# Issuing the loads of the keys ahead of the reciprocals' store and load in step 4 of the first layer

## The chip, the cores and the metric

The program runs on one core of one Trainium2 chip. The metric is the device time of one execution in microseconds; the median of a few executions is given. The core has five instruction queues that run side by side: TensorE (PE), VectorE (DVE), ScalarE (ACT), GpSimd (POOL) and SyncE (SP). SP here only issues DMA transfers and waits on semaphores. Each queue runs its own instructions strictly in order.

## The reference

Two transformer layers run one after the other on x of shape (8, 512, 128), each with a modulation from a small vector c. The first layer, in which the change lies, is an attention with 16 heads of 8 elements, followed by a routed feed-forward block:

```python
mod = (_silu(L0_c) @ L0_wmod).reshape(8, 6, 1, -1)      # sa, ca, ga, sb, cb, gb
h = _layernorm(x) * (1 + ca) + sa
latent = h @ Wc_down
q = (latent @ Wq_up).reshape(B, T, 16, 8)
k, v = split(latent @ Wkv_up)                           # one key/value head of 8, shared by all 16
att = softmax(causal(einsum('bthd,bsd->bhts', q, k) / sqrt(8)))
y = einsum('bhts,bsd->bthd', att, v).reshape(B, T, 128)
x = x + ga * (y @ Wc_proj)
h = _layernorm(x) * (1 + cb) + sb
x = x + gb * experts(h)          # 8 experts, each takes its 1024 best tokens
```

The second layer is a windowed attention (64 tokens) and a gated token-mixing block. All inputs and outputs are float32.

## The kernel before

The attention of the first layer is a software pipeline over the 8 batch rows. Every engine runs the same double loop, `for n in range(-2, 9)` and, inside, `for s in range(10)`; n is a pass, s a step. In pass n, row n has its scores, exponentials and products with the values computed, one 128x128 block of (queries, keys) in each of the ten steps. At the same time row n+1 has its maxima finished, row n+2 is projected to queries and keys, and row n-1 has its outputs normalised, projected and added to X.

[...]

- **Queries and keys of row n+2.** PE projects the queries in step 1 and the keys in step 2 (`q`, `k` in `misc`, L485 and L488). Each is cut into three bf16 parts by ACT, DVE and POOL (tiles `qs` and `ks`). In step 3 SP stores both to DRAM (`d_q<-qs` L1102, three transfers; `d_k<-ks` L1106, four). In step 4 ACT issues the three loads of the queries (`Q<-d_q`, L666, 384 KB each) and SP the three loads of the keys (`K<-d_k`, L1143, 24 KB each). The two sets count on one semaphore, `q_in`. PE waits for it before the first product of the maxima of that row (L462), which stands at the start of step 8 of the same pass.
- **Maxima of row n+1.** PE multiplies Q and K (L462, with the mask L469), DVE reduces (L798). In step 6 PE transposes the result (L496), DVE cuts it into parts `ms` (L763 to L767), SP stores it (`d_m<-ms` L1163), waits until the store has landed, and loads it as three rows of Q (`Q<-d_m` L1167). PE waits for these rows (`m_in`) before the first scores of the next pass (L423).
- **Sums of row n-1.** SP loads the sums of the exponentials (`lc<-d_y` L1121) and the outputs (`yt<-d_y` L1123) in step 0. DVE takes reciprocals in step 3 (`rc`, L905). In step 4 SP stores them (`d_r<-rc` L1130), waits until the store has landed (L1131), and loads them spread over the partitions (`rl<-d_r` L1132). POOL multiplies in step 6 (`yn`, L1053), PE projects near the end of step 8 (`pj`, L501), DVE adds to X (L770) and, in passes up to 4, takes the statistics of row n+3 (L739). From these POOL makes the normalised row (L1014, L983), which PE transposes in step 0 of the next pass (L480).
- **Outputs of row n.** ACT copies them out of PSUM (L637) after steps 0, 2, 5 and 9; SP stores each copy in the step after (`y_store`, L1088). In steps 1, 3 and 6, and in step 0 of the next pass, there is such a store; in step 4 there is none.

The order on SP is the order in which its loop is written. In step 4 of passes 1 to 5 it is: the reciprocals' store, the wait, the reciprocals' load, then a wait for the keys' stores (`k_st`) and the three loads of the keys. Passes -2 to 0 have keys to load but no reciprocals; passes 6 and 7 have reciprocals but no keys. In step 5 SP loads `cb` (L1154), in step 6 it does an outputs' store and the transfers of the maxima.

Of the kernel before, what the change touches and what calls it, by code (L numbers as in the profile page):

```python
# [27 lines left out]
NB, T, D = 8, 512, 128  # L28
NT = T // P
NTILE = NB * NT  # L30
NH, DH = 16, 8
# [8 lines left out]
PARTS = 3  # L40
# [4 lines left out]
QB = 3  # L45
# [136 lines left out]
def program(nc, ctx, ins, out):  # L182
# [3 lines left out]
    def sem(name):  # L186
        return ctx.enter_context(nc.semaphore(name))
# [7 lines left out]
    def sb0(name, shape, dt=F32):  # L195
        return a0.enter_context(nc.sbuf_tensor(name, shape, dt))

    def dram(name, shape, dt):
        return nc.dram_tensor(name, shape, dt, kind="Internal").ap()
# [3 lines left out]
    d_k = [dram(f"d_k{i}", [PARTS, DH, T], BF16) for i in range(2)]  # L203
# [58 lines left out]
    K = [sb0(f"K{i}", [P, T], BF16) for i in range(QB)]  # L262
# [57 lines left out]
    DS = {n: sem("a0_" + n) for n in dnames}  # L320
# [42 lines left out]
    def bc(ap, shape):  # L363
        return ap.to_broadcast(shape)
# [704 lines left out]
    def sync_part(sp):  # L1069
# [11 lines left out]
        def y_store(Y):  # L1081
            b, g = divmod(Y, NT)
            sp.wait_ge(S["y_ev"], Y + 1)
            if g == 0 and b >= 2:
                sp.wait_ge(DS["yt_in"], 16 * (b - 1))
                sp.wait_ge(DS["lc_in"], 16 * (b - 1))
            for j in range(4):
                sp.dma_start(d_y[b % 2][4 * j:4 * j + 4, :, P * g:P * g + P].rearrange("h d q -> d h q"),  # L1088
                             ysb[Y % 2][32 * j:32 * j + DH + 1, :].rearrange("p (h q) -> p h q", q=P)
                             ).then_inc(DS[f"y_st{Y % 2}"], 16)  # L1090

        for n in range(-LEAD, NB + TAIL):
            for s in range(NSTEP):
                t = NSTEP * n + s
                b = n + 2
                if 0 <= b < NB and s == 3:
                    par = b % 2
                    sp.wait_ge(S["q3_rdy"], b + 1)
                    if b >= 2:
                        sp.wait_ge(DS[f"q_in{par}"], QIN * (b // 2))  # L1100
                    for a in range(PARTS):
                        sp.dma_start(bass.AP(d_q[par].tensor, a * D * T, [[T, NH], [NH * T, DH], [1, T]]),  # L1102
                                     qs[:, a, :]).then_inc(DS[f"q_st{par}"], 16)
                    sp.wait_ge(S["k3_rdy"], b + 1)
                    for i in range(NT):
                        sp.dma_start(bass.AP(d_k[par].tensor, P * i, [[T, DH], [DH * T, PARTS], [1, P]]),  # L1106
                                     ks[32 * i:32 * i + DH, :, :]).then_inc(DS[f"k_st{par}"], 16)
                if 0 <= t - 1 < NSTEP * NB:
                    b, ps = divmod(t - 1, NSTEP)
                    g, i = STEPS[ps]  # L1110
                    if g == i and b < LB:
                        y_store(NT * b + g)
                b = n - 1
                if 0 <= b < LB and s == 0:
                    for par in range(2):
                        sp.wait_ge(DS[f"y_st{par}"], 64 * 2 * (b + 1))
                    if b >= 1:
                        sp.wait_ge(S["rc_rdy"], b)
                        sp.wait_ge(S["yn_rdy"], b)
                    y = d_y[b % 2]  # L1120
                    sp.dma_start(lc[:, :], bass.AP(y.tensor, DH * T, [[(DH + 1) * T, NH], [64, T // 64], [1, 64]])  # L1121
                                 ).then_inc(DS["lc_in"], 16)
                    sp.dma_start(yt[:, :], bass.AP(y.tensor, 0, [[(DH + 1) * T, NH], [T, DH], [1, T]])  # L1123
                                 ).then_inc(DS["yt_in"], 16)
                if 0 <= b < LB and s == 4:
                    sp.wait_ge(S["rc_rdy"], b + 1)
                    if b >= 2:
                        sp.wait_ge(DS["rl_in"], 16 * (b - 1))
                    r = d_r[b % 2]
                    sp.dma_start(r.rearrange("h (a q) -> (h a) q", q=64), rc[:, :]).then_inc(DS["r_st"], 16)  # L1130
                    sp.wait_ge(DS["r_st"], 16 * (b + 1))  # L1131
                    sp.dma_start(rl[:, :], bass.AP(r.tensor, 0, [[T, NH], [0, DH], [1, T]])).then_inc(DS["rl_in"], 16)  # L1132
                if (n, s) in LIMIT_ROWS:
                    i = LIMIT_ROWS.index((n, s))
                    sp.wait_ge(s_eye, 1)
                    sp.dma_start(K[i][NPR:P, :], KC[:, :]).then_inc(s_kc[i], 16)
                    sp.dma_start(Q[i][P - QW:P, :, :], bc(QC[:, :].unsqueeze(1), [QW, NH, T])).then_inc(s_kc[i], 16)
                b = n + 2
                if 0 <= b < NB and s == 4:
                    par = b % 2  # L1140
                    sp.wait_ge(DS[f"k_st{par}"], 64 * (b // 2 + 1))
                    for c in range(PARTS):
                        sp.dma_start(K[b % QB][24 * c:24 * c + 24, :],  # L1143
                                     bass.AP(d_k[par].tensor, c * DH * T, [[0, PARTS], [T, DH], [1, T]])
                                     ).then_inc(DS[f"q_in{par}"], 16)
                if n == -1 and s == 3:
                    sp.wait_ge(s_modR, 2)
                    sp.dma_start(d_cb, modR[:, 0, 2 * D:5 * D]).then_inc(DS["cb_st"], 16)
                if 0 <= n < NB and s == 5:
                    if n == 0:  # L1150
                        sp.wait_ge(DS["cb_st"], 16)
                    if n >= 2:
                        sp.wait_ge(S["h2_rdy"], n - 1)
                    sp.dma_start(cb[n % 2][:, :, :].rearrange("p a d -> p (a d)"),  # L1154
                                 bass.AP(d_cb.tensor, 3 * D * n, [[0, P], [1, 3 * D]])).then_inc(DS[f"cb_in{n % 2}"], 16)
                b = n + 1
                if 0 <= b < NB and s == 6:
                    par = b % 2
                    sp.wait_ge(S["m_rdy"], b + 1)
                    if b >= 2:  # L1160
                        sp.wait_ge(DS[f"m_in{par}"], 48 * (b // 2))
                    for a in range(PARTS):
                        sp.dma_start(bass.AP(d_m[par].tensor, a * NH * T, [[QW, NQB], [4 * T, NHG], [T, 4], [1, QW]]),  # L1163
                                     ms[:, a, :]).then_inc(DS["m_st"], 16)
                    sp.wait_ge(DS["m_st"], 16 * PARTS * (b + 1))
                    for a in range(PARTS):
                        sp.dma_start(Q[b % QB][NPR + a:NPR + a + 1, :, :], d_m[par][a:a + 1, :, :]  # L1167
                                     ).then_inc(DS[f"m_in{par}"], 16)
                if (s == 7 and 0 <= n - 2 < LB - 2) or (n, s) in ((LB, 4), (NB, 0)):
                    b = n - 2  # L1170
                    sp.wait_ge(S["misc_free"], M0.full(("h2", b)))
                    sp.dma_start(d_hT[:, T * b:T * b + T], h2T[:, :]).then_inc(DS["h_st"], 16)
                if 0 <= n < NB and s == 9:
                    for dst, src in late_weights[n::NB]:
                        sp.dma_start(dst, src, allow_slow_non_contiguous=True).then_inc(s_lw, 16)
                    if n == 0:
                        sp.dma_start(d_acc.rearrange("(i p) d -> p i d", p=P),
                                     bc(zrow[:, :].unsqueeze(1), [P, NTILE, D])).then_inc(s_lw, 16)
                b = n - 2
                if 0 <= b < LB and s == 9:  # L1180
                    sp.wait_ge(S["tab_rdy"], b + 1)
                    sp.dma_start(d_tab[T * b:T * b + T, :].rearrange("(i p) f -> p i f", p=P),
                                 tab[:, :, :]).then_inc(DS["tab_st"], 16)
# [38 lines left out]
    g.zrow, g.biti, g.bitf = zrow, biti, bitf  # L1222
    g.WT, g.GG, g.WPG, g.WVG, g.BPG, g.m1, g.gmean = WT, GG, WPG, WVG, BPG, m1, gmean
    stages = [(tensor_part, scalar_part, vector_part, gpsimd_part, sync_part), moe(nc, ctx, g)]
    mid.close()
    stages.append(block1(nc, ctx, g, out))
# [1260 lines left out]
```

## Time and profile before

| | us |
|---|---|
| median of 3 runs | 889.79 |
| lowest and highest | 885.54 and 890.29 |
| the profiled execution | 883.99 |
| its span, first to last instruction | 882.2 |

| engine | busy us | share |
|---|---|---|
| PE | 730.6 | 83% |
| DVE | 561.2 | 64% |
| ACT | 450.2 | 51% |
| POOL | 400.6 | 45% |

The attention of the first layer fills the span up to about 380 us; the experts follow up to about 640 us, then the second layer. A wait is listed by the instruction that waited and by what it waited for. A transfer lands when its semaphore shows it complete. PEclk is the clock that was granted to TensorE, as a share of 2.4 GHz; at 0.5 it is at its lower level of 1.2 GHz. The profiled execution is 1.8 us longer than its span.

### The profile page before, as it was taken

To read this page: it belongs to the slowest core of one execution; us is meant where nothing else is said; L and a number is where in the kernel's file an instruction comes from. 1 tells how busy PE (TensorE), PEld (TensorE's weight loads), DVE (VectorE), ACT (ScalarE), POOL (GpSimd) and SP (SyncE) were. 2 spreads that over 40 slices of the span, in tenths; PEclk is the share of its full clock that TensorE was granted. 3 is DMA by queue.
4 is the path that set the end of the run, shared out by engine and by line. 5 is a ranking of instruction groups with operands and counts; after the bars stand their busy time and mean duration, and the time that the engine had idled before them with its cause. 6 is when DMAs were issued, how large, how long until landed. Compare 5 with 4: busy or idle time off the path is not lost.

```text
span 882.2 us, 22943 instructions
## 1 busy us (share of the span) xinstructions
PE 730.6 (83%) x9158; PEld 384.5 (44%) x9158; DVE 561.2 (64%) x1506; ACT 450.2 (51%) x742; POOL 400.6 (45%) x531
## 2 busy tenths in 40 slices
PE   4588896999898898948889978899947699999887
PEld 2234343444444443323334434444424356556555
DVE  4877675878686775466763423302287688888884
ACT  2013664666575657713225423333346588888663
POOL 5021022524233232210036888887545669885333
PEclk9756998999999999969999978899957799999999
DMA  6621454256543432230011333333300111111001
GB/s 164 130 56 32 96 153 98 58 124 178 103 97 92 96 80 72 79 105 39 0 26 45 43 40 44 45 45 33 50 25 2 25 27 25 38 26 26 18 22 37
DMA packets 73924, 55.06 MB, mean 62 GB/s; under 512 B 23699, under 2 KB 66819, under 8 KB 73219
## 3 DMA queue, kind: packets, MB, share of 16 engines
q1 hardware_dynamic: 63098, 36.58, 16.3%
q0 software_dynamic: 9856, 7.58, 6.7%
q10 hardware_dynamic: 864, 9.44, 5.1%
q8 instruction: 73, 1.20, 0.6%
q14 instruction: 33, 0.26, 0.1%
HBM read 31.76 MB, written 18.23 MB: 57 GB/s over the span
## 4 chain that ended last, share of the span: by engine, by line
PE 42%; DVE 19%; DMA 12%; issue 7%; POOL 6%; SPq 6%; ACT 5%; another core or an unknown queue 1%; POOLq 1%; DVEq 0%; ACTq 0%
PE ps_o L1585 6%; DMA d_r<-rc 4%; PE bank L462 3%; PE b1ps L2075 3%; PE b1ps L2086 3%; PE ps_s L423 3%; DVE R L1477 3%; PE bank L439 3%; DVE MX L798 3%; POOL d_acc L1381 3%; PE ps_h L1573 3%; DMA K<-d_k 2%; PE b1ps L2099 2%; POOL xn L983 2%; SPq L1088 2%
## 5 line engine op out<-in xcount | busy, mean ns | idle before, releaser
L798 DVE TENSOR_REDUCE MX<-bank 128x1 f32<-128x320 f32 (+13 forms) x352 | 180.8, 562 | 56.6 <-PE bank L469 54.2
L649 ACT ACTIVATE PR<-ps_s 128x1024 f32<-128x1024 f32 x160 | 155.7, 1022 | 107.7 <-PE ps_s L419 65.5
L462 PE MATMUL bank<-K,Q 72*32 72x32 bf16 (+15 forms) x2048 | 122.6, 314 | 37.6 <-DMA K<-d_k 23.3
L462 PEld LDWEIGHTS bank<-K,Q 72*32 72x32 bf16 x2048 | 49.6, 106 | 125.4 <-DVE MX L798 60.1
L423 PE MATMUL ps_s<-Q,K 97*32 97x512 bf16 (+1 forms) x1088 | 96.1, 386 | 5.6 <-DMA Q<-d_m 4.7
L1381 POOL DMA_INDIRECT d_acc<-Y,idx x56 | 87.7, 1566 | 20.7 <-issue 16.2
L1371 POOL DMA_INDIRECT XG<-d_tab,idx x56 | 53.9, 963 | 78.2 <-DVE idx L1486 60.6
L439 PE MATMUL bank<-PR,VE 128*32 128x512 f32 x640 | 87.6, 625 | 0.0
L1585 PE MATMUL ps_o<-H,w 128*128 128x512 f32 x176 | 86.4, 641 | 0.0
L1705 ACT ACTIVATE H<-ps_h,b1T 128x512 f32<-128x512 f32 x88 | 60.3, 687 | 43.9 <-PE ps_h L1573 31.4
L469 PE MATMUL bank<-maskQ,identb 128*32 128x32 bf16 (+3 forms) x1408 | 73.3, 201 | 0.0
L1518 DVE TENSOR_TENSOR Y<-ps_o,XG 128x512 f32<-128x512 f32 x14 | 9.7, 692 | 85.3 <-PE ps_o L1592 80.9
L1573 PE MATMUL ps_h<-XT,w 128*128 128x512 f32 x112 | 54.3, 607 | 3.1 <-issue 1.8
L2202 ACT ACTIVATE PT<-b1ps 128x512 f32<-128x512 f32 x64 | 38.1, 596 | 32.0 <-PE b1ps L2086 31.5
L1585 PEld LDWEIGHTS ps_o<-H,w 128*128 128x128 f32 x176 | 34.9, 206 | 39.9 <-issue 39.2
L469 PEld LDWEIGHTS bank<-maskQ,identb 128*32 128x32 bf16 x1408 | 40.0, 103 | 17.6 <-issue 9.6
L2207 ACT ACTIVATE PB<-SU 128x512 f32<-128x512 f32 x64 | 40.2, 628 | 13.7 <-DVE SU L2274 13.2
L1053 POOL TENSOR_TENSOR yn<-yt,rl 128x512 f32<-128x512 f32 x7 | 8.9, 1271 | 83.7 <-issue 65.9
L2274 DVE TENSOR_TENSOR SU<-b1ps,mxs 128x512 f32<-128x512 f32 x64 | 44.3, 692 | 2.2
L983 POOL TENSOR_SCALAR xn<-X,mv,rs 128x128 f32<-128x128 f32 x56 | 44.7, 810 | 1.5
L2075 PE MATMUL b1ps<-KB,QT 64*32 64x512 f32 x512 | 36.6, 629 | 9.2 <-DMA KB<-KT 5.4
L2271 DVE TENSOR_REDUCE mxs<-b1ps 128x8 f32<-128x512 f32 x64 | 43.3, 677 | 0.6 <-PE b1ps L2075 0.6
(347 smaller groups left out, 1375.7 us busy)
## 6 DMA issues: line engine op xcount, KB each, us to landing
Q<-d_q ACTq DMA_DIRECT2D x24, 384.0 KB
d_q<-qs SPq DMA_DIRECT2D x24, 128.0 KB, 2.7
X<-L_attn_x SPq DMA_DIRECT2D x8, 256.0 KB, 5.0
w<-L_ffn_W SPq DMA_DIRECT2D x8, 256.0 KB, 4.3
d_acc<-zrow SPq DMA_DIRECT2D x1, 2048.0 KB, 11.2
w<-L_ffn_W SPq DMA_DIRECT2D x1, 2048.0 KB, 9.7
AC<-d_acc SPq DMA_DIRECT2D x8, 256.0 KB, 3.0
d_y<-ysb SPq DMA_DIRECT2D x112, 18.0 KB
```

The source lines that it names most:

```text
L423: last = nc.tensor.matmul(out_, k_[0:r, P * i + o:P * i + o + QW], q_[0:r, :, P * g + QW * j:P * g + QW * j + QW], start=True, stop=True, ...
L439: last = nc.tensor.matmul(ps_y[32 * j:32 * j + 32, :], VE[b % QB][:, i, :], PR[t % 2][:, j, :], start=(i == 0), stop=(i == g), tile_positi ...
L462: nc.tensor.matmul(mx[o:o + QW, x * w:(x + 1) * w], Q[b % QB][0:NPR, 4 * c + hh, QW * j:QW * j + QW], K[b % QB][0:NPR, 0:w], start=(x == 0 ...
L469: last = nc.tensor.matmul(diag[o:o + QW], identb[:, o:o + QW], bc(maskQ[:, :].unsqueeze(1), [P, len(cs), QW]), start=False, stop=True, til ...
L649: nc.scalar.activation(by_head.rearrange("p h (c x) -> p c h x", x=QW), ps_s[half][:, :].rearrange("p (c h x) -> p c h x", c=2, x=QW), ACT ...
L798: nc.vector.tensor_reduce(MX[b % 2][:, c:c + len(cs)], ring[R0.place["max", G]][:, 0:len(cs) * w].rearrange("p (x w) -> p x w", w=w), AX_X ...
L983: last = nc.gpsimd.tensor_scalar(dst[:, i, :], src[:, i, :], m_[:, i, 0:1], r_[:, i:i + 1], ALU.subtract, ALU.mult)
L1381: nc.gpsimd.indirect_dma_start(out=g.d_acc, out_offset=bass.IndirectOffsetOnAxis(ap=idx[:, rx + 1, k:k + 1], axis=0), in_=Y[rx % 2][:, k, ...
L1573: T_.matmul(ps_h[u % 2][:, :], g.w1[:, e, P * c:P * c + P], rows[:, 512 * h:512 * h + 512], start=True, stop=True).then_inc(h_ps, 1)
L1585: last = T_.matmul(ps_o[h][:, :], g.w2[:, ITS[it], c, :], H[h][:, c, :], start=(c == 0), stop=(c == NC_DI - 1))
L1705: nc.scalar.activation(H[h][:, c, :], ps_h[u % 2][:, :], ACT.Gelu, bias=g.b1T[:, ITS[it], c:c + 1]).then_inc(h_cp, 1)
L2075: last = T_.matmul(ps_s[(U + hh) % SB][32 * j:32 * j + 32, :], QT[b % 2][64 * hh:64 * hh + 64, q:q + 32], KB[b % 2][64 * hh:64 * hh + 64, ...
```

## The change

The block of SP that waits for `k_st` and issues the three loads of the keys moves up in the loop body. It stood behind the outputs' store, the loads of step 0, the reciprocals' store and load, and the constant rows; it now stands right behind the stores of the queries and keys of step 3.

```diff
@@ -1105,6 +1105,14 @@
                         sp.dma_start(bass.AP(d_k[par].tensor, P * i, [[T, DH], [DH * T, PARTS], [1, P]]),
                                      ks[32 * i:32 * i + DH, :, :]).then_inc(DS[f"k_st{par}"], 16)
+                b = n + 2
+                if 0 <= b < NB and s == 4:
+                    par = b % 2
+                    sp.wait_ge(DS[f"k_st{par}"], 64 * (b // 2 + 1))
+                    for c in range(PARTS):
+                        sp.dma_start(K[b % QB][24 * c:24 * c + 24, :],
+                                     bass.AP(d_k[par].tensor, c * DH * T, [[0, PARTS], [T, DH], [1, T]])
+                                     ).then_inc(DS[f"q_in{par}"], 16)
                 if 0 <= t - 1 < NSTEP * NB:
...
@@ -1135,14 +1143,6 @@
-                b = n + 2
-                if 0 <= b < NB and s == 4:
-                    par = b % 2
-                    sp.wait_ge(DS[f"k_st{par}"], 64 * (b // 2 + 1))
-                    for c in range(PARTS):
-                        sp.dma_start(K[b % QB][24 * c:24 * c + 24, :],
-                                     bass.AP(d_k[par].tensor, c * DH * T, [[0, PARTS], [T, DH], [1, T]])
-                                     ).then_inc(DS[f"q_in{par}"], 16)
```

No other engine's program changes.

## Rows read from the trace of the kernel before

**Rows 1.** The page, part 4: shares of the span in the chain that ended last.
```profile
PE ps_o L1585 6%; DMA d_r<-rc 4%; PE bank L462 3%; PE b1ps L2075 3%; PE b1ps L2086 3%; PE ps_s L423 3%; DVE R L1477 3%; PE bank L439 3%; DVE MX L798 3%; POOL d_acc L1381 3%; PE ps_h L1573 3%; DMA K<-d_k 2%; PE b1ps L2099 2%; POOL xn L983 2%; SPq L1088 2%
```
**Rows 2.** Line L1143, 120 to 330 us: who waited for the keys (us, times).
```profile
  PE bank L462: 12.8, 5
```
**Rows 3.** Timeline of PE, passes 1 to 3: start, us, instruction [idle before].
```profile
149.99 0.30 PE L462 MATMUL bank<-K,Q 72*32 72x32 bf16 x16 [6.40 <-DMA K<-d_k]
188.78 0.28 PE L462 MATMUL bank<-K,Q 72*32 72x32 bf16 x16 [0.34 <-DMA K<-d_k]
228.89 0.30 PE L462 MATMUL bank<-K,Q 72*32 72x32 bf16 x16 [1.45 <-DMA K<-d_k]
```
**Rows 4.** Timeline of SP, pass 3.
```profile
214.39 1.39 SPq L1088 DMA_DIRECT2D d_y<-ysb  x4
216.74 0.35 SPq L1130 DMA_DIRECT2D d_r<-rc  x1
224.07 0.56 SPq L1132 DMA_DIRECT2D rl<-d_r  x1
224.69 2.30 SPq L1143 DMA_DIRECT2D K<-d_k  x3
227.37 0.36 SPq L1154 DMA_DIRECT2D cb<-d_cb  x1
229.34 1.91 SPq L1163 DMA_DIRECT2D d_m<-ms  x3
232.60 0.82 SPq L1167 DMA_DIRECT2D Q<-d_m  x3
```
**Rows 5.** Timeline of SP, passes 1 and 2.
```profile
145.30 0.56 SPq L1132 DMA_DIRECT2D rl<-d_r  x1
...
193.14 0.82 SPq L1167 DMA_DIRECT2D Q<-d_m  x3
```
**Rows 6.** Line L1130, 120 to 330 us: five stores of the reciprocals.
```profile
DMA to landing us min/median/max: 5.1/7.3/9.8
```
**Rows 7.** Stretches of pass 3: PE, PEld, DVE, ACT, POOL busy, PEclk, DMA share, GB/s.
```profile
222.00:224.00 2.00, 1.97 (x33) 0.61 (x25) 1.66 (x3) 1.96 (x3) 0.00 (x0) 1.00 0.85 180
224.00:226.00 2.00, 2.00 (x27) 0.74 (x26) 1.07 (x4) 1.79 (x3) 0.00 (x0) 1.00 0.23 78
228.00:233.00 5.00, 4.11 (x113) 2.42 (x113) 1.94 (x4) 1.66 (x3) 0.81 (x1) 0.66 0.31 73
```
**Rows 8.** Timeline, pass 0: keys' loads, queries' loads, first product.
```profile
95.65 2.66 SPq L1143 DMA_DIRECT2D K<-d_k  x3
95.89 0.30 ACTq L666 DMA_DIRECT2D Q<-d_q  x1
...
108.59 0.28 PE L462 MATMUL bank<-K,Q 72*32 72x32 bf16 x16 [3.34 <-DMA Q<-d_q]
```
**Rows 9.** Timeline of POOL and PE, passes 2 and 3: projection of the outputs.
```profile
227.54 1.27 POOL L1053 TENSOR_TENSOR yn<-yt,rl 128x512 f32<-128x512 f32 x1 [11.94 <-issue]
...
191.28 1.16 PE L501 MATMUL bank<-wg,yn 128*128 128x128 f32 x8
...
232.97 1.16 PE L501 MATMUL bank<-wg,yn 128*128 128x128 f32 x8
```
**Rows 10.** Timeline of PE: first scores of passes 3, 4 and 6.
```profile
197.34 0.39 PE L423 MATMUL ps_s<-Q,K 128*32 128x512 bf16 x1 [1.35 <-DMA Q<-d_m]
237.51 0.38 PE L423 MATMUL ps_s<-Q,K 128*32 128x512 bf16 x1
318.52 0.39 PE L423 MATMUL ps_s<-Q,K 128*32 128x512 bf16 x1 [0.23 <-DMA Q<-d_m]
```
**Rows 11.** Timeline of PE: next query projection, passes 3 and 4.
```profile
205.38 1.10 PE L485 MATMUL bank<-hT,w_fold 128*128 128x512 f32 x2
245.02 1.10 PE L485 MATMUL bank<-hT,w_fold 128*128 128x512 f32 x2
```

## The prediction, made before the changed kernel was run

> **What bounds the kernel now.** I read the page's chain first. It spends 4% of the span (35 us) on the reciprocals' store `d_r<-rc` and 2% on the keys' loads [rows 1]: 32 KB and 72 KB a pass, in a kernel whose chain otherwise consists of matmuls. Next the question who waits for the keys: in passes 1 to 5 it is the first product of the maxima, five times and 12.8 us in all [rows 2]. The timeline of PE shows each wait: 6.40 us in pass 1, 0.34 in pass 2, 1.45 in pass 3 [rows 3]; the remaining 4.6 belong to passes 4 and 5. Last the timeline of SP in pass 3 [rows 4]. The outputs' store ends at 215.78. The reciprocals' store is issued at 216.74, and SP then stands until 224.07, because it must have landed before it is loaded again. Only then are the keys loaded, and PE starts at 228.89. That store takes 5.1 to 9.8 us to land [rows 6]. The DMA engines are 85% busy just before it lands and 23% busy just after [rows 7]; what keeps them busy are the queries' loads, 1.15 MB issued at about the same time. So the keys stand behind a small store that itself stands in a crowd.
>
> A gap of PE costs twice. The granted clock over 228 to 233 us is 0.66 [rows 7], so part of that stretch ran at 1.2 GHz, where the clock had been 1.00 until 226. From the first product to the projection of the outputs PE needs 2.50 us in pass 2, after a gap of 0.34, and 4.08 in pass 3, after 1.45 [rows 3, 9].
>
> **The change, part by part.** *What it moves past.* No outputs' store falls in step 4, so on the way up the keys' block passes only the reciprocals' store, its wait and its load, in passes 1 to 5. In passes -2 to 0 the order of SP stays as it is, and passes 6 and 7 load no keys.
>
> *The keys earlier.* Pass 0 already has the new order. There the keys were issued at 95.65, right after an outputs' store, and no wait for their own stores shows [rows 8]. In pass 3 they can start at 215.8 in place of 224.69, 8.9 us earlier. PE would want them at 228.89 - 1.45 = 227.44. They share the engines with the queries' loads, which seem to end at about 225 [rows 7], so I count the keys as there in time. If nothing else were late, the gain would be the waits, 12.8, and the slow clock after four of them, 4 x (4.08 - 2.50) = 6.3: 19 us.
>
> *The reciprocals later.* Issuing the three loads takes SP 2.30 us [rows 4], so the store goes out at 218.15, 1.4 later. It cannot be sooner than before; with an unchanged flight its load is 1.4 later, and the landing may be held up more, since the keys' data is in front of it in SP's queue. At the other end, pass 0: its queries were issued at 95.89 and PE got them at 108.59, 12.7 us later, with the keys beside them [rows 8]. A reciprocals' store that lands only when such a stream ends would land, in pass 3, at 215.82 + 0.24 + 12.7 = 228.8, 4.7 late. I take 2.4, nearer to the first, as the queries' stream of pass 3 has been shorter than that of pass 0. For pass 1 I take 0.5: it had the longest flight, so it landed with the end of the stream already.
>
> *Who waits for that, first POOL and PE.* `yn` starts 3.47 us after the load is issued (224.07 to 227.54) and takes 1.27 [rows 4, 9]; with 2.4 more it is ready at 231.2. PE, freed of the gap and at full clock, arrives at the projection L501 at 227.44 + 2.50 = 229.9. It waits 1.3 us, and starts 1.8 earlier than 232.97.
>
> *Then SP itself.* After the reciprocals' load come the `cb` load, an outputs' store and the round trip of the maxima. The keys' block, 224.69 to 227.37 = 2.7 us, is gone from there, but everything stands d later. So `Q<-d_m` moves by d - 2.7: 0.3 earlier in pass 3. From the end of its issue to PE's start it took 197.34 - (193.14 + 0.82) = 3.4 [rows 5, 10]. In pass 3 it was issued until 233.42, so it landed at about 236.8, and PE used it at 237.51: a slack of 0.7. After passes 2 and 5 PE already waited for it, 1.35 and 0.23 us [rows 10]. This is the wait that takes the place of the old one.
>
> *The sum.* At the first scores of the next pass the gain is: pass 1, 2.7 - 0.5 = 2.2; pass 2, 0.3; passes 3 and 4, 0.7 + 0.3 = 1.0 each; pass 5, 0.3. Together 4.8. Each new wait may slow the clock as the old one did. Pass 3 began after 1.35 us of waiting and needed 8.04 us from its first scores to the projection of queries; pass 4 began without and needed 7.51 [rows 10, 11]. That is 0.53, in four places where it was not before: 2.1. Net 2.7 us. In the profiled execution's terms 883.99 becomes 881.3. That execution lies 5.8 below the median of the runs shown, and I take the difference from the median: 889.79 - 2.7 = 887.1. The later layers are not touched; their work follows a shift one to one.
>
> *A rule weighed.* The row first: a store of 32 KB took up to 9.8 us to land beside the queries' loads, which come from ACT's queue [rows 6]. The Trainium skill, DMA: Bandwidth & Descriptors, section Queues, rings and completion order, says that each DMA engine serves its queue rows in turn, one packet of several descriptors each time. By that rule three more transfers in front of the reciprocals' store cost it further turns of the queries, and a short flight turns into a long one; the sum would then be that of the slower rival below. By the row alone, which has a flight of 5.1 to 9.8 without the keys in front, nothing says which it will be.
>
> **The rivals.**
>
> *Only `yn` limits.* `Q<-d_m` comes sooner than I reckon, as its issue and the store before it find a quieter queue. Then the gain is that at L501: 1.8 in passes 3, 4 and 5, none in pass 2, and in pass 1 154.1 (149.99 + 4.08) less 150.5 (145.30 + 0.5 + 3.47 + 1.27) = 3.6. Sum 9.0: 880.8. For it: the keys' loads themselves were in the air while these small transfers were issued. Against: SP's serial work from the reciprocals' load to `Q<-d_m` is visible and does not shrink.
>
> *All of it comes back*, 19 us: 870.8. It needs the reciprocals to be no later at all in all passes.
>
> *Slower: the round trip of the reciprocals lengthens by more than the keys' block.* The place is SP's wait at L1131, the price d - 2.7 for `Q<-d_m`. With d = 4.7 it lands 2.0 later. Passes 3 and 4 lose 2.0 - 0.7 + 0.5 = 1.8 each, pass 2 2.0 and pass 5 2.5, pass 1 nothing: 8 us, 897.9. The queries would reach PE at 228.8, so that even the old gap stayed. It decides at d = 2.7 in passes 2 and 5, and at 3.4 in passes 3 and 4. For it: pass 0, and the shared engines. Against: pass 0 also carried other loads of SP through the same stretch, which stay behind the wait here.
>
> *Nothing happens*, 889.8: keys and queries land together, later than today's keys need, and what is late now is the queries' loads.
>
> **How the numbers follow.** The forecast has 0.46, only `yn` 0.22, all of it 0.06, slower 0.16, nothing 0.10. This measurement can tell about 0.5%, 4.4 us, from no change. Faster by more than that are the second and third cases and 0.08 of the forecast: 0.36. Slower are most of the slower case: 0.13. The same: 0.51. The forecast's own range is 884 to 890. The full one reaches from 878, past the case of `yn` alone, to 894, into the slower case; outside are the full gain and about half of the slower one.
>
> **What would show it.** In SP's timeline of passes 1 to 5 the keys' loads start right after the outputs' store, and `rl<-d_r` is issued 1.4 to 3.4 later than before against its pass, in pass 1 under 1. PE no longer lists `K<-d_k` for these passes, but waits for POOL's `yn` at L501 and for `Q<-d_m` at L423 in nearly all. The chain still holds `d_r<-rc`. I am wrong if PE waits for `Q<-d_q` or the keys at L462 for more than 1 us in passes 2 to 5 (the queries' stream is longer), if neither of the two new waits shows (then the gain is near 19), or if the passes get longer from first scores to first scores.

## The result, and the profile after

| | before | changed |
|---|---|---|
| median | 886.05 us (20 runs) | 892.86 us (20 runs) |
| ratio | | 1.007, 95% interval 1.0042 to 1.0098 |
| the profiled execution | 883.99 us | 884.29 us |

The changed kernel is 0.7% slower, about 6 us, where 2.7 us less had been forecast. Two repeats in other sets of runs gave 0.998 (0.993 to 1.003) and 1.0067 (1.0037 to 1.0096), so two of three measurements say 0.7% and one could not tell it from nothing. Ratios leave disturbed executions out, and so differ a little from those of the medians, and two of the profiles below (the changed order without the round trip, and reciprocals earlier with the keys last) are of such executions.

SP's timeline of pass 3 of the changed kernel, to be held against [rows 4]:

```profile
212.42 1.39 SPq L1088 DMA_DIRECT2D d_y<-ysb  x4
213.85 2.27 SPq L1113 DMA_DIRECT2D K<-d_k  x3
216.23 0.51 SPq L1138 DMA_DIRECT2D d_r<-rc  x1
225.95 0.58 SPq L1140 DMA_DIRECT2D rl<-d_r  x1
226.91 0.34 SPq L1154 DMA_DIRECT2D cb<-d_cb  x1
229.18 1.91 SPq L1163 DMA_DIRECT2D d_m<-ms  x3
232.44 0.81 SPq L1167 DMA_DIRECT2D Q<-d_m  x3
```

The keys go out 0.04 us after the outputs' store; before, 8.9 us after it. The reciprocals' load goes out 12.1 us after it (225.95 - 213.81); before, 8.3. Who waits on PE in passes 1 to 5 (126 to 325 us; us in total, times, longest), and SP at the reciprocals' load, in the kernel before:

```profile
PE bank L462 <- DMA K<-d_k: 12.8, 5, 6.4
PE ps_s L423 <- DMA Q<-d_m: 1.6, 2, 1.3
...
SPq L1132 <- DMA d_r<-rc: 36.1, 5, 9.5
```

and the changed one:

```profile
PE bank L501 <- POOL yn L1053: 11.2, 5, 2.8
PE bank L462 <- DMA K<-d_k: 2.8, 2, 2.5
PE bank L462 <- DMA Q<-d_q: 2.1, 1, 2.1
...
SPq L1140 <- DMA d_r<-rc: 45.7, 5, 10.8
```

Ten of the 12.8 us of waiting for keys are gone, but 2.1 us of waiting for the queries stand at the same instruction in pass 5, and 11.2 us of waiting for `yn` have come. PE's timeline of passes 2 and 3 shows the place, to be held against [rows 3, 9, 10]:

```profile
185.18 0.28 PE L462 MATMUL bank<-K,Q 72*32 72x32 bf16 x16
...
190.32 2.05 PE L501 MATMUL bank<-wg,yn 128*128 128x128 f32 x8 [2.56 <-POOL yn L1053]
...
225.79 0.28 PE L462 MATMUL bank<-K,Q 72*32 72x32 bf16 x16 [0.32 <-DMA K<-d_k]
...
231.09 2.05 PE L501 MATMUL bank<-wg,yn 128*128 128x128 f32 x8 [2.71 <-POOL yn L1053]
...
236.82 0.39 PE L423 MATMUL ps_s<-Q,K 128*32 128x512 bf16 x1
```

The reader is to see two things. The gap has moved 5 us down PE's program, from L462 to L501. And the eight projections take 2.05 us where they took 1.16 in both passes before: the clock is low there now. The stretch of 231 to 234 us has it (columns as in [rows 7]):

```profile
231.00:234.00 3.00, 2.91 (x24) 2.23 (x28) 0.83 (x2) 0.00 (x0) 0.00 (x0) 0.50 0.17 27
```

0.50 is 1.2 GHz, after a gap of 2.7 us. From L501 to the first scores of the next pass PE needed 232.97 to 237.51 = 4.54 us before, and 231.09 to 236.82 = 5.73 now, at these clocks (before, then changed):

```profile
232.97:237.51 4.54, 4.39 (x110) 2.72 (x105) 3.97 (x14) 1.94 (x2) 1.05 (x2) 1.00 0.57 85
231.09:236.82 5.73, 5.70 (x100) 3.83 (x100) 3.61 (x14) 1.94 (x2) 1.27 (x2) 0.71 0.41 74
```

Not every pass is like this one. Over passes 1 to 5 of the three profiles of the change, the granted clock of this stretch was 0.55 to 0.72 in twelve cases of fifteen and 1.00 in three. In the two profiles of the kernel before it was 0.94 to 1.00 in seven of ten and 0.85 to 0.88 in the other three.

In this profile the page's chain no longer names the keys or the reciprocals' store (in the second and third profile of the change it names the store again, with 3% and 2%). The wait for them lies in the "issue" in front of `yn` (chain in order of time: start, us, what):

```profile
213.48 0.14 SPq L1088
213.63 15.94 issue
229.57 1.27 POOL yn L1053
230.84 0.24 issue
231.09 2.06 PE bank L501 x8
```

### The profile page after: what moved, and what is told of

Same layout as the page of the kernel before. It is cut to its first block, busy times and chain, and to the rows that moved or that the text cites. A ratio compares the mean times of both kernels' runs of the same rounds, so it can differ in the third digit from the quotient of the medians.

```text
span 882.5 us, 22943 instructions
## 1 busy us (share of the span) xinstructions
PE 731.0 (83%) x9158; PEld 386.0 (44%) x9158; DVE 560.4 (63%) x1506; ACT 449.9 (51%) x742; POOL 400.5 (45%) x531
## 4 chain that ended last, share of the span: by engine, by line
PE 31%; POOL 19%; issue 16%; DVE 15%; DMA 7%; SPq 6%; ACT 5%; POOLq 1%; DVEq 0%; ACTq 0%
POOL d_acc L1381 8%; POOL XG L1371 4%; PE b1ps L2075 3%; PE b1ps L2086 3%; POOL xn L983 3%; PE ps_s L423 2%; DVE MX L798 2%; PE bank L439 2%; PE ps_o L1585 2%; PE bank L462 2%; PE b1ps L2099 2%; PE ps_h L1573 2%; SPq L1088 2%; DVE hit L1415 1%; SPq L1102 1%
## 5 line engine op out<-in xcount | busy, mean ns | idle before, releaser
L462 PE MATMUL bank<-K,Q 72*32 72x32 bf16 (+15 forms) x2048 | 121.0, 309 | 28.6 <-DMA K<-d_k 13.6
L423 PE MATMUL ps_s<-Q,K 97*32 97x512 bf16 (+1 forms) x1088 | 98.0, 389 | 6.3 <-DMA Q<-d_m 5.7
L462 PEld LDWEIGHTS bank<-K,Q 72*32 72x32 bf16 x2048 | 48.8, 103 | 113.6 <-DVE MX L798 54.8
L1585 PE MATMUL ps_o<-H,w 128*128 128x512 f32 x176 | 90.5, 666 | 0.0
L439 PE MATMUL bank<-PR,VE 128*32 128x512 f32 x640 | 85.5, 612 | 0.0
```

The costliest lines, as they stand in the source:

```text
L423: last = nc.tensor.matmul(out_, k_[0:r, P * i + o:P * i + o + QW], q_[0:r, :, P * g + QW * j:P * g + QW * j + QW], start=True, stop=True, ...
L439: last = nc.tensor.matmul(ps_y[32 * j:32 * j + 32, :], VE[b % QB][:, i, :], PR[t % 2][:, j, :], start=(i == 0), stop=(i == g), tile_positi ...
L462: nc.tensor.matmul(mx[o:o + QW, x * w:(x + 1) * w], Q[b % QB][0:NPR, 4 * c + hh, QW * j:QW * j + QW], K[b % QB][0:NPR, 0:w], start=(x == 0 ...
L1585: last = T_.matmul(ps_o[h][:, :], g.w2[:, ITS[it], c, :], H[h][:, c, :], start=(c == 0), stop=(c == NC_DI - 1))
```

## The experiments

Theory R: the price is the reciprocals' round trip, which the change makes later, and `yn` with it. Theory C: the keys' data crowds the queries' loads. "d" is, as in the prediction, how much later the reciprocals' load is issued than in the kernel before, counted from the end of the outputs' store of step 3.

**Second and third measurement of the change.**

> The changed kernel once more, for a second profiled execution and its times beside the kernels of the same call. Theory R (the reciprocals' round trip): 5 to 7 us slower than the kernel before; in passes 1 to 5 the reciprocals' store takes 9 to 11 us to land, and PE waits 1.3 to 2.8 us for yn at L501 in each, as in the first profile of the changed kernel. Theory C (the crowd: the keys' data slows the queries' loads): 5 to 7 us slower as well, but the waits are mostly for the queries at L462 (1 to 3 us a pass). Theory N (the attention is not what moved the median): the attention ends within 3 us of the kernel before in this profile too, and the later layers carry the difference.

Measured: 891.75 against 890.25, ratio 0.998 (0.993 to 1.003). The ratio is below what both theories expected. The store took 7.2 to 9.6 us, 8.5 on average, where R had 9 to 11. The waits of passes 1 to 5 are R's in the main (0.4 to 3.7 us each, so not all within R's 1.3 to 2.8):

```profile
PE bank L501 <- POOL yn L1053: 12.0, 5, 3.7
...
PE bank L462 <- DMA Q<-d_q: 0.2, 1, 0.2
```

The queries have 0.2 us, where C wanted 1 to 3 a pass. Theory N's sign is there as well: the attention ends within 0.3 us of the kernel before in this profile (391.26 against 391.48). It is not in the next one, which ends it at 397.94.

> The changed kernel a third time. Two measurements gave a ratio of 1.007 and of 0.998. Theory R has it between: the sum of 4 us gained in pass 1 and 1 to 2 us lost in each of passes 2 to 5, so 0 to 4 us slower than the kernel before; waits for yn at L501 in at least four of the five passes.

Measured: 891.59 against 886.56, ratio 1.0067 (1.0037 to 1.0096), 5 us and so a little over the expected 0 to 4.

```profile
PE bank L501 <- POOL yn L1053: 12.2, 5, 3.5
...
PE bank L462 <- DMA Q<-d_q: 2.4, 1, 2.4
```

The wait for `yn` stands in all five passes of all three profiles, at 11 to 12 us in all. In the three, d of passes 2 to 5 is 4.3, 3.4 and 4.5 on average (12.1, 11.2 and 12.3 us from outputs' store to reciprocals' load, against 7.8), that of pass 1 1.6, -0.3 and 1.9.

**The kernel before again.**

> The kernel before once more, for a second profiled execution. Flights of the reciprocals' store of 5 to 10 us, waits for the keys at L462 in passes 1 to 5 of 10 to 15 us in all, none for yn.

Measured: 885.79 us (one execution), the waits as expected.

```profile
PE bank L462 <- DMA K<-d_k: 12.2, 5, 3.7
```

The five single waits differ (pass 1 had 6.4 us in the first profile and 3.7 here), their sum hardly; from the outputs' store to the reciprocals' load passes 2 to 5 took 8.1 us on average. So 7.8 was no accident. Pass 1 is another matter: its 9.9 us of the first profile are 8.0 here.

**Store, keys, wait, load.** Only the place of the keys differs from the kernel before, and only the place of the reciprocals' store from the changed one:

```diff
                     sp.dma_start(r.rearrange("h (a q) -> (h a) q", q=64), rc[:, :]).then_inc(DS["r_st"], 16)
+                    if n + 2 < NB:
+                        keys_load(n + 2)        # wait for k_st, three loads
                     sp.wait_ge(DS["r_st"], 16 * (b + 1))
                     sp.dma_start(rl[:, :], ...).then_inc(DS["rl_in"], 16)
```

> Passes 1 to 5, step 4 of SP: reciprocals' store, keys' loads, wait for the store, reciprocals' load. The store keeps its place in front of SP's queue, and the keys are issued in the time in which SP would only wait. Theory R: the store lands 5 to 10 us after its issue as before, yn is as early as before, the keys' gap is gone; 4 to 9 us faster than the kernel before, no wait for yn over 1 us. Theory C: the keys still travel with the queries, so the queries land 1 to 2 us later and it is as slow as the change, 3 to 7 us slower than before.

Measured: 883.48 against 890.25, ratio 0.993 (0.989 to 0.997).

> Store, keys, wait, load once more: 0.3 to 1.1% faster than the kernel before again, and slower than the version with the reciprocals a step earlier by 2 to 6 us.

Measured: 875.32 against 886.56, ratio 0.988 (0.985 to 0.991), a little more than the expected 0.3 to 1.1%. It was not slower than the version with the reciprocals a step earlier (873.65 in the same set); that expectation missed. Pass 3 of SP in the first profile:

```profile
211.48 0.35 SPq L1138 DMA_DIRECT2D d_r<-rc  x1
211.89 2.26 SPq L1096 DMA_DIRECT2D K<-d_k  x3
220.63 0.58 SPq L1142 DMA_DIRECT2D rl<-d_r  x1
```

and the waits of passes 1 to 5:

```profile
PE ps_s L423 <- DMA Q<-d_m: 5.3, 4, 1.9
PE bank L501 <- POOL yn L1053: 2.7, 2, 1.7
PE bank L462 <- DMA K<-d_k: 2.6, 2, 1.8
```

The keys are issued 0.4 us behind the store, 0.7 to 1.7 us behind the first of the queries' loads (in the change 0.6 us ahead of it to 1.3 behind), so their data travels with the queries' here too; yet this is faster than before by 0.7 and 1.2%. That speaks against theory C. Waits for `yn` have not gone quite: two, of up to 1.7 us, where R allowed none over 1. The distance from outputs' store to reciprocals' load is 7.5 us in passes 2 to 5, the old one: d = 0. The wait that now comes last is `Q<-d_m` (7.9 us in the second profile of this kernel), the one the forecast had seen for the change.

**Without the round trip.** The load into `rl` reads the input x and waits for nothing (the outputs are scaled by wrong values):

```diff
-                    sp.wait_ge(DS["r_st"], 16 * (b + 1))
-                    sp.dma_start(rl[:, :], bass.AP(r.tensor, 0, ...)).then_inc(DS["rl_in"], 16)
+                    sp.dma_start(rl[:, :], bass.AP(ins["L0_attn_x"].tensor, 0, ...)).then_inc(DS["rl_in"], 16)
```

> The changed order, but the load into rl reads the input x in place of the stored reciprocals and does not wait for their store (the first layer's attention outputs are scaled by wrong values). Theory R: without that wait neither yn nor the maxima's round trip is late: 8 to 19 us faster than the kernel before. Theory C: the crowd is larger still, as 256 KB more are in it; PE waits for the queries 1 to 3 us a pass, and it is no faster than the kernel before.

> The order of the kernel before, with rl loaded from x and no wait, as in the run above (the same part is wrong). The keys are then issued behind a 256 KB load, but 7 us sooner than before. Theory R: within 3 us of the run above, 8 to 19 us faster than the kernel before, since it is the wait and not the order that costs. Theory C: no faster than the kernel before.

Measured: 0.989 (0.983 to 0.995) in the changed order, 0.993 (0.988 to 0.997) in the old. Both are faster than before, 9.9 and 6.5 us of 890: the first inside R's span, the second 1.5 us short of it. In neither profile does PE wait for `yn` at all. In the changed order L462 keeps

```profile
PE bank L462 <- DMA K<-d_k: 3.9, 2, 2.6
...
PE bank L462 <- DMA Q<-d_q: 1.4, 1, 1.4
```

The keys' loads stand to the queries' as in the change, and theory C, which wanted no gain here, falls. With the wait gone the change is no loss, and which of the two stands first makes no difference that these intervals can tell.

**The change in pass 1 only, and in passes 2 to 5 only.**

```diff
+                if 0 <= n + 2 < NB and s == 4 and (n == 1):      # the other kernel: n != 1
+                    keys_load(n + 2)
```

The old place keeps the other passes; passes -2 to 0 have the same order at either place.

> The keys' loads ahead of the reciprocals in pass 1 alone. Theory R: pass 1 had the longest flight already, so it loses little there and gains 3 to 4 us of its gap of 6.4: 2 to 4 us faster than the kernel before, and passes 2 to 5 as before. Theory C: 0 to 2 us slower.

> The keys' loads ahead of the reciprocals in passes 2 to 5 alone. Theory R: each of these passes loses 0 to 2 us to the wait for yn at L501 and the slow clock after it: 3 to 8 us slower than the kernel before, slower than the change itself by the 3 to 4 us of pass 1. Theory C: 4 to 6 us slower, the waits being for the queries at L462.

Measured against 886.59: pass 1 only 886.21, ratio 1.002 (0.998 to 1.005); passes 2 to 5 only 889.47, ratio 1.0066 (1.0023 to 1.0109). The change in passes 2 to 5 alone has the loss, 3 us by the medians and 6 by the ratio; in pass 1 alone none can be told. The expected gain of 2 to 4 us in pass 1 does not show, and with it falls the expectation that passes 2 to 5 alone would be 3 to 4 us slower than the whole change: the two ratios are 1.0066 and 1.007, from different sets. The profile says why: the wait for the keys in pass 1 was 6.4 and 3.7 us in the two profiles before and is 2.1 here, and 3.5 for `yn` came.

```profile
PE bank L501 <- POOL yn L1053: 3.5, 1, 3.5
PE bank L462 <- DMA K<-d_k: 2.1, 1, 2.1
```

In passes 2 to 5 of the other kernel (165 to 325 us):

```profile
PE bank L501 <- POOL yn L1053: 8.0, 4, 2.6
PE ps_s L423 <- DMA Q<-d_m: 3.9, 3, 1.6
```

**The reciprocals a step earlier.** VectorE takes them in step 2, SP stores them behind the keys' stores of step 3, ahead of the outputs' store; in step 4 come keys, wait, load.

```diff
-                if 0 <= b < LB and s == 3:
+                if 0 <= b < LB and s == 2:
                     dve.wait_ge(DS["lc_in"], 16 * (b + 1))
...
+                b = n - 1
+                if 0 <= b < LB and s == 3:
+                    sp.wait_ge(S["rc_rdy"], b + 1)
...
+                    sp.dma_start(r.rearrange("h (a q) -> (h a) q", q=64), rc[:, :]).then_inc(DS["r_st"], 16)
```

> VectorE takes the reciprocals in step 2 instead of 3, SP stores them right behind the keys' stores of step 3 (before the outputs' store), and in step 4 issues the keys' loads first, then the wait and the reciprocals' load. The store leaves about 2 us before the queries' loads start. Theory R (the round trip in the crowd is the price): its flight drops from 5 to 11 us to 2 to 4, rl is loaded about 3 us sooner than in the kernel before, no wait for yn at L501, keys' gap gone: 8 to 16 us faster than the kernel before, and at least as fast as the run with store, keys, wait, load. Theory C (the crowd itself): the 256 KB of rl are now in the queries' stream, PE waits for the queries 1 to 3 us a pass, and it is not faster than the kernel before.

> The version with the reciprocals a step earlier and the keys first, once more beside the others of this call: 0.7 to 1.5% faster than the kernel before again.

Measured: 874.66 against 886.59, ratio 0.989 (0.985 to 0.993), and 873.65 against 886.56, ratio 0.989 (0.985 to 0.993). SP in pass 3, and the waits of passes 1 to 5:

```profile
211.37 0.35 SPq L1122 DMA_DIRECT2D d_r<-rc  x1
211.76 1.45 SPq L1088 DMA_DIRECT2D d_y<-ysb  x4
213.25 2.25 SPq L1096 DMA_DIRECT2D K<-d_k  x3
215.55 0.58 SPq L1145 DMA_DIRECT2D rl<-d_r  x1
```

```profile
PE bank L462 <- DMA K<-d_k: 5.0, 3, 3.2
PE ps_s L423 <- DMA Q<-d_m: 0.4, 1, 0.4
```

SP does not wait for the store at all now: it has landed while the keys were issued. The 256 KB of `rl` go out right into the queries' loads, and no wait for the queries shows; the keys are still waited for, 5.0 us in all.

**The same, keys last.** In step 4: wait, reciprocals' load, keys' loads.

> Reciprocals taken in step 2 and stored in step 3 as in the run with the reciprocals a step earlier, but in step 4 SP keeps the old order: wait, reciprocals' load, keys' loads. Theory R: the order of keys and reciprocals matters only because of the long wait between them. With a flight of 2 to 4 us the wait is under 2 us, the keys go out at about 219 where the kernel before sent them at 225: 7 to 13 us faster than the kernel before, within 4 us of the version with the keys first. A rival O (the keys have to be first in SP's queue to come in front of the queries): 0 to 3 us faster than before only, with waits for the keys at L462 of 1 us or more a pass.

Measured: 876.01 against 886.56, ratio 0.990 (0.986 to 0.993).

```profile
213.76 0.35 SPq L1122 DMA_DIRECT2D d_r<-rc  x1
214.15 1.44 SPq L1088 DMA_DIRECT2D d_y<-ysb  x4
215.64 0.56 SPq L1143 DMA_DIRECT2D rl<-d_r  x1
216.25 2.24 SPq L1096 DMA_DIRECT2D K<-d_k  x3
```

Store to load is 1.9 us. Once the store's flight does not lie in the queries' loads, no difference can be told between the two orders of keys and reciprocals (0.989 and 0.990). Rival O falls by its time, 0 to 3 us faster at most; the waits it named are there in part (6.4 us for the keys in all, over 1 us in three passes, against 5.0 with the keys first).

## Why the prediction was wrong

**Right:** the block passes only the reciprocals' store, wait and load; the keys start right behind the outputs' store and the wait for them shrinks (12.8 us to 2.8, 2.3 and 4.0 in the three profiles); a wait for `yn` at L501 comes in its place; the clock falls after it. The cause of the slower rival, a round trip that lengthens by more than it gives back, is the one that came. Two of the signs of being wrong that the prediction named came as well: passes 2 to 5 got longer, and PE waited over 1 us for the queries at L462 in one pass each of two of the three profiles (2.1 and 2.4 us).

**The step that failed is "The reciprocals later".** The forecast took d = 2.4 in passes 2 to 5 and 0.5 in pass 1. The three profiles of the change have 4.1 (mean of 4.3, 3.4 and 4.5) and 1.1 against the first profile before; against the second they have 3.8 and 3.0. So in passes 2 to 5 d came near the forecast's upper value of 4.7, not its lower one of 1.4. And the 0.5 of pass 1 rested on one long flight, 9.85 us, which was 7.65 in the second profile.

Some 1.5 to 2.3 us of d is the issue of the keys; 1.4 had been reckoned for pass 3, and 1.46 was measured there. The rest is a longer flight: the five stores took 7.7 us on average from issue to the load behind them in the kernel before, and 9.6, 8.5 and 9.8 in the change, where the forecast had granted one more microsecond. Store, keys, wait, load has 7.4 and 7.8 with the same data in the air.

*Why the flight is longer.* Two things differ for the store in the change: the keys are in front of it on its own queue, and it goes out 1.8 to 3.6 us behind the first of the queries' three loads, when all of them have been issued. With the keys not in front it mostly goes out between them. The rows are of pass 3 of the first profile before, where the store's own line is in [rows 4],

```profile
216.43 0.30 ACTq L666 DMA_DIRECT2D Q<-d_q  x1
216.76 0.80 ACTq L666 DMA_DIRECT2D Q<-d_q  x2
```

and of pass 3 of the second, where it came later:

```profile
215.37 0.31 ACTq L666 DMA_DIRECT2D Q<-d_q  x1
215.72 0.87 ACTq L666 DMA_DIRECT2D Q<-d_q  x2
216.54 0.35 SPq L1130 DMA_DIRECT2D d_r<-rc  x1
```

The first flew 7.3 us, the second 8.7. In the profiles with no keys in front of the store (two of the kernel before, two of store, keys, wait, load, and the unchanged passes of the two partial kernels), the twenty that went out 0.3 to 0.4 us behind the first of the queries' loads took 7.0 us on average (5.1 to 9.4). The five that went out 0.6 to 1.3 us behind it took 9.3 (8.7 to 9.9). The fifteen of the change took 9.3 too (7.2 to 11.8). So the place behind the queries' loads goes with the longer flight even with no keys in front, and that the keys in front add anything is not shown. The rule of the Trainium skill weighed in the prediction (DMA: Bandwidth & Descriptors, Queues, rings and completion order) gave the keys in front a price, further turns of the queries; these runs do not show such a price apart from that of going out later. No run sent the store out later without the keys in front on purpose.

**What follows from d = 4.1 at L501.** `yn` was ready at 228.81 in pass 3 and used at 232.97 [rows 9], a slack of 4.16: nothing is left to gain. The other slacks, by the same two instructions of the first profile before, are 0.85 in pass 2 (190.43 to 191.28), 3.7 in pass 4 and 4.0 in pass 5, and 4.4 in pass 1. By this sum pass 2 loses 3.2, passes 3 to 5 lose 0.4 in all, pass 1 gains 3.3: the gain is zero. The forecast worked out the slack of pass 3 alone; its rival with `yn` as the only limit has "none in pass 2", where it was a loss.

The sum is right in total, not pass by pass. From first scores to first scores, the mean of the three profiles of the change less the mean of the two before is -0.2 us in pass 1 and +1.3, +0.5, +0.6 and +0.2 in passes 2 to 5. Pass 1 shows no gain; the 3.3 rest on the long flight of the first profile. And in pass 2 of that profile `yn` had started 6.3 us after its load was issued (182.86 to 189.15), not the 3.47 of pass 3, so it moved by less than the load did.

**The second miss is the clock.** Its price was put at 0.53 us after `Q<-d_m`, 2.1 in all. It fell at L501: 1.19 us (5.73 less 4.54) in pass 3. Over passes 1 to 5, from L501 to the next first scores took 24.4 and 26.9 us in the two profiles before and 27.0, 28.1 and 31.1 in the change, so 3.0 more on average, though PE waits less there for `Q<-d_m`. The gap before L462 had cost 1.6 for the slow clock, but that gain sits ahead of L501 and is eaten by the wait there.

**The place of the slower rival was off.** It was to act through `Q<-d_m`, from d = 2.7 on. That wait is 0 to 1.8 us in all in the change; L501 takes the delay first. `Q<-d_m` is what is late once the reciprocals are on time: 5.3 us in store, keys, wait, load.

**What stays open.** These terms add up to 3 us, and the attention of the change ended 2.4 us later in the first profile (experts' first load at 393.86 against 391.48), with 391.3 and 397.9 in its other two and 393.1 in the second of before. The measured 5 to 6 us of two sets are more than that, and the third set has none. Passes 2 to 5 took 163.4, 159.6 and 165.6 us in the change against 159.7 and 160.7 before. From the first scores of pass 6, where the change touches nothing, to the end of the attention it was 75.5, 75.5 and 74.9 against 73.0 and 73.9; other kernels here have 73.3 to 76.6, so this may be scatter, and no run explains it. Five profiles of single executions don't settle the size. That the delayed round trip brings the loss is shown by the two kernels that take it out: with the store ahead of the keys, and with no wait for the store, the loss becomes a gain. That passes 2 to 5 alone have the loss, and the wait for `yn`, is shown too.

## What to carry to other kernels

A queue that waits for a round trip is best filled during the wait: issue the store, then whatever else is ready, then wait. Putting the ready work ahead of the store moves the whole round trip, and the later end of it belongs to someone else. Before such a swap, look up for each pass how early the displaced result is today (here 0.85 to 4.4 us), in more than one profile, and price its delay as issue time plus a longer flight. To start the small store before the large loads begin gave 1.0 to 1.1% here, whatever the order of the rest; that it beats filling the wait (0.7 and 1.2%) is not shown.

## What the runs showed of the hardware

- A 32 KB store issued 0.3 to 0.4 us behind the first of three loads on another queue, 1.15 MB together, needed 5.1 to 9.4 us (7.0 on average), and 0.6 to 1.3 us behind it 8.7 to 9.9. One issued 1.5 to 1.6 us ahead of them was through in 1.9 to 2.1. With 72 KB of loads ahead of it on its own queue, and 1.8 to 3.6 us behind the first of the large loads, it needed 7.2 to 11.8.
- In the three profiles of the change PE waited for the queries, loaded with the keys' 72 KB beside them, 0.2 to 2.4 us over all five passes.
- After gaps of 2.6 and 2.7 us of TensorE eight 128x128 fp32 products took 2.05 us in place of 1.16, at a granted clock of 0.50. The gap alone does not decide it: in the second profile of the change they took 1.13 us after a gap of 2.55 (pass 3), at a granted clock of 1.00.
